# Second layer's convolution: offsets in two halves of the columns, the channel-major image in planes of contiguous tokens, the image scaled after its projection, expert masks made in pairs, base points moved

## The chip, the cores and the metric

One core of a Trainium2 chip runs the whole program. The metric is the device time of one execution in microseconds (us). The kernel before takes 274.34 us, the median of three runs (274.07 to 274.48). The engines are named as the profile names them: PE (TensorE, matmuls; PEld is its weight loads), DVE (VectorE), ACT (ScalarE), POOL (GpSimd), SP (SyncE, which here issues all DMAs).

## The reference, cut to what matters

A block of two layers works on x of 4 images, 16 x 16 tokens, 64 channels. Each layer is a deformable convolution and then a mixture of experts, each on a layer norm of its input and added to it. The change concerns the second layer's convolution and the steps on either side of it:

```
x = x + _L1_conv_ref(_ln_c(x), ...)          # _ln_c: (v - mean) / sqrt(var + 1e-6) over the channels
# inside _L1_conv_ref
x = conv_same(x, w_init, b_init)             # 1 x 1, 64 -> 64: "the image"
for g in range(4):                           # groups of 16 channels
    offsets = conv_same(xi, w_off[g], b_off[g])      # 3 x 3, 16 -> 18: nine points (x, y) for each token
    sampled = sample_with_offsets(xi, offsets, 3)    # bilinear, nine points for each token
    h = depthwise_same(sampled, w_dw[g], b_dw[g])
    outs.append(conv_same(h, w_pw[g], b_pw[g]))
```

Before it stands the first layer's mixture (eight experts, the two best weighted, gelu), after it the second's (the best expert alone, relu, with a capacity).

## The kernel before, in words

The 1024 tokens lie as 128 partitions x 8 columns (J = 8): a partition is half a row of an image, a column is one of the eight tokens of that half row. "Half" below means columns 0 to 3 or 4 to 7. Each engine runs its own hand-written list of instructions and meets the others at semaphores; nothing reorders a list. Where a helper records an operation, the profile gives the helper's line.

Around the change the order is this.

* First mixture. PE makes hidden rows (L840), broadcasts gate weights (L848), sums outputs (L862). ACT does the gelu (L645). DVE multiplies hidden rows by gates (L1425), sixteen times. Ahead of the sixteen, DVE adds the partition's position to the sampling base points (L1414, two instructions).
* Image. DVE adds the mixture's output to x in two halves (L1418), takes moments, POOL takes the power for the inverse deviation (L435), DVE normalises (L1128), PE transposes (L725), ACT copies. Then PE makes the image twice: channel-major in one matmul for each half (L910), copied by ACT and DVE into a padded picture (L251), and token-major (L754), copied by ACT in one piece (L660). SP stores it to a zeroed padded scratch in memory with four DMAs (L350) and reads back, with eight DMAs (L362), a window of five rows x twelve columns for each half row.
* Offsets. PE convolves the padded picture (L928: three taps for all tokens on 128 rows, three on 64 rows, in two blocks of 512 tokens). ACT adds the bias (L664), PE turns the result to tokens (L941).
* Weights. DVE adds base points, clips and subtracts (L1446 to L1451), ACT makes the linear tents (L669 to L676), DVE makes nine tables of weights, one for each of 3 x 3 neighbours (L282), each when its two factors are there. DVE then finishes a flag (L1145, L1146): if an offset is larger than one token, a general branch would run instead. It is not taken here.
* Sampling. Twelve items: four pairs of columns x three rows of sample points. For each item nine products of a slab and a table are summed. POOL makes six of the nine (L265, 72 in all), DVE three (L265, 36 in all). PE sums three of POOL's and one of DVE's in PSUM (L960), DVE adds the other five (L1555, L1559, L1564). POOL has eight slots for its products, and takes one again when PE or DVE has summed what lay there. PE then transposes the samples (L968) and applies the fused depthwise and pointwise weights (L978, L986).
* Second mixture. PE broadcasts one-hot masks (L1049), DVE masks the inputs (L1603), PE makes the hidden rows of the chosen expert (L1058), then outputs (L1098); DVE and POOL weigh and join them.

Some matmuls on zeros (L716, L708) compute nothing: `idle_columns` and `keep_clock` issue them so that PE is not idle. Thirty-two of them stand between L941 and the sampling.

Of the kernel before, what the change touches and what calls it, by code (L numbers as in the profile page):

```python
# [38 lines left out]
K = 9  # L39
# [31 lines left out]
def program(nc, a, out):  # L71
    ctx = ExitStack()
    with ctx:
# [13 lines left out]
        pad0, pad1 = scratch("pad0", R0), scratch("pad1", R1)  # L87
# [55 lines left out]
        w_i1 = sb("w_i1", P, 2, C)  # L143
# [99 lines left out]
        assert UE + G1 * UW <= BIG, UE + G1 * UW  # L243

        block = ctx.enter_context(nc.Block())

        def pad_image(copy, n):

            for hf in range(2):
                for b in range(B):  # L250
                    last = copy(V(cpad1, C * hf, b * NP0 + (W + 2) * (1 - hf) + 1 + HJ * n,  # L251
                                  [[1, C], [1, HJ], [W + 2, H], [HC, 2]]),
                                bank(4 + n, C * hf, C * hf + C, [P, HJ], [2, H], [1, 2], off=32 * b))
            return last
# [20 lines left out]
        def x_tents1(dx):  # L275

            return bank(4 + dx, 0, P, [1, J * GP1])

        def pair_weights(eng, d):

            dy, dx = divmod(d, 3)
            eng.tensor_tensor(bigv(AD + d * J * GP1, [1, J * GP1]), bigv(T1 + dy * J * GP1, [1, J * GP1]),  # L282
                              x_tents1(dx), ALU.mult).then_inc(sem("pairs"), 1)
# [22 lines left out]
        def _(sp):  # L306
# [14 lines left out]
            for pad, reach in ((pad0, R0), (pad1, R1)):  # L321
                n = B * (H + 2 * reach) * (W + 2 * reach) * C // P
                sp.dma_start(V2(pad, [[n, P], [1, n]]), zero[:, 0:n]).then_inc(sem("pad_zeroed"), 16)
# [8 lines left out]
            for i in range(2):  # L332
                load(w_i1[0:C + 1, i, :], "w_i1", "w_i1")
            load(w_of[:, 0, :], "w_of_a", "w_of")
            for hf in range(2):
                load(w_of[C * hf:C * hf + C, 1, :], "w_of_b", "w_of")
# [4 lines left out]
            load(b_tb[C:C + 1, :], "b_pw", "w_dp")  # L341

# [57 lines left out]
            sp.wait_ge(sem("img1"), 1)  # L400
            image_out(pad1, R1, "img1", "pad1_stored")
            slabs_in(pad1, R1, "pad1_stored", "slab1")
# [10 lines left out]
        def _(pool):  # L413
# [28 lines left out]
            for weights in (w_i1[:, :, :], cw_parts[:, :, :], oh_parts[:, :, :], b1_parts[:, :]):  # L442
                last = gp.memset(weights, 0.0)
# [29 lines left out]
            gp.memset(V(cpad1, 0, 0, [[1, P], [1, B * NP0]]), 0.0).then_inc(sem("cpad1_zero"), 1)  # L473
# [21 lines left out]
            pool.wait_ge(sem("w_of"), 64)  # L495
# [64 lines left out]
        def _(act):  # L560
            sc = nc.scalar

            def copy_T(k, halves=range(2)):

                for h in halves:
                    act.wait_ge(sem("xT_ps"), 2 * k + h - 1)
                    twice = {3: XT2, 5: XN2}
# [82 lines left out]
            for hf in range(2):  # L650
                act.wait_ge(sem("y0_ps"), hf + 1)
                sc.copy(bigv(Y0 + 512 * hf, [1, 512]), bank(4 + hf, 0, P, [1, 512])).then_inc(sem("yT0"), 1)
                if hf == 0:
                    copy_T(4, [0])

            act.wait_ge(sem("imgT_ps"), 1)
            pad_image(sc.copy, 0).then_inc(sem("cpad1"), 1)
            copy_T(4, [1])
            act.wait_ge(sem("img1_ps"), 2)
            sc.copy(V(img, 0, 0, [[1, P], [256, 2], [1, 256]]), bank(2, 0, P, [512, 2], [1, 256])).then_inc(sem("img1"), 1)  # L660
            act.wait_ge(sem("w_of"), 64)
            for n in range(2):
                act.wait_ge(sem("offT_ps"), n + 1)
                sc.activation(offT[:, 512 * n:512 * n + 512], bank(n, 0, 72, [1, 512]), ACT.Identity, bias=b_of[:, 0:1]  # L664
                              ).then_inc(sem("offT"), 1)

            NX = J * GP1
            act.wait_ge(sem("off1"), 1)
            sc.activation(x_tents1(2), u1[:, 0:NX], ACT.Relu).then_inc(sem("tent_x1"), 1)  # L669
            sc.activation(loc1[:, :], u1[:, :], ACT.Abs).then_inc(sem("abs1"), 1)  # L670
            act.wait_ge(sem("abs1"), 1)
            sc.activation(x_tents1(1), loc1[:, 0:NX], ACT.Relu, bias=1.0, scale=-1.0).then_inc(sem("tent_x1"), 1)
            sc.activation(x_tents1(0), u1[:, 0:NX], ACT.Relu, scale=-1.0).then_inc(sem("tent_x1"), 1)
            sc.activation(loc1[:, NX:2 * NX], loc1[:, NX:2 * NX], ACT.Relu, bias=1.0, scale=-1.0
                          ).then_inc(sem("tent_y1"), 1)
            sc.activation(ml[:, 0:NX], u1[:, NX:2 * NX], ACT.Relu, scale=-1.0).then_inc(sem("tent_y1"), 1)  # L676
# [10 lines left out]
            copy_raw_T(1)  # L687
            copy_T(5, [0])
# [3 lines left out]
            copy_T(5, [1])  # L692
# [8 lines left out]
        def _(pe):  # L701
# [17 lines left out]
            def transposes(k, src, ready, done_before, halves=range(2), m=C):  # L719

                pe.wait_ge(sem("ident"), 1)
                for h in halves:
# [4 lines left out]
                    if h == halves[0] and k in IDLE_BETWEEN:  # L727
                        idle_columns(*IDLE_BETWEEN[k])

            def gate_logits(src, ready, w, done_before):  # L730

                for h in range(2):
                    pe.wait_ge(sem(ready), h + 1)
# [1158 lines left out]
```

## Time and profile before

| | us |
|---|---|
| median of three runs | 274.34 |
| the profiled execution | 273.77 |
| its span, first to last instruction | 272.0 |
| PE busy | 230.9 (85%) |
| DVE busy | 191.2 (70%) |
| POOL busy | 136.6 (50%) |
| ACT busy | 60.2 (22%) |

The span leaves out 1.77 us of the profiled execution's time. The mean granted clock of TensorE is 0.986 of full speed. The shares of busy time are averages over stages that have different limits; the chain of work that ended last says, stage by stage, which engine the next step waited for.

### The profile page before, as it was taken

Reading aid. Unit: us, or ns where it says so; the run is one execution under the profiler, and the core shown is the slowest. Engines: PE = TensorE matmul, PEld = TensorE weight load, DVE = VectorE, ACT = ScalarE, POOL = GpSimd, SP = SyncE. Lnnn points to the kernel's source line nnn. Section 1 sums busy time; section 2 is a strip of 40 time slices with the busy share of each in tenths; the row PEclk is TensorE's granted clock in tenths of the full one; section 3 lists DMA queues with packets and bytes.
Section 4 is the critical chain, followed back from the end, with each engine's and each line's share of the span. In section 5 each row is a group of like instructions: output and inputs, shape, how many; then the busy total and the mean of one; then the engine's idle time right before and its main releaser. Section 6 shows DMA issues by size and latency. Waiting matters only on the chain.

```text
span 272.0 us, 3157 instructions
## 1 busy us (share of the span) xinstructions
PE 230.9 (85%) x1006; PEld 131.3 (48%) x1011; DVE 191.2 (70%) x480; ACT 60.2 (22%) x102; POOL 136.6 (50%) x195
## 2 busy tenths in 40 slices
PE   0999988987999979979798777789899988999980
PEld 0736467863345623224524233557577856434430
DVE  7797889997894886473506799898877138425486
ACT  1221953210001282614114000101001212311000
POOL 5400009885990619712600899999997002000760
PEclk9999999999999889999999999999999999999996
DMA  3526991000000000000059000000000000000000
GB/s 93 173 69 147 208 227 70 0 2 0 2 0 1 2 1 1 0 0 2 0 123 202 2 4 0 0 2 0 2 0 0 0 2 1 0 2 0 0 19 19
DMA packets 5760, 9.39 MB, mean 35 GB/s; under 512 B 2390, under 2 KB 2926, under 8 KB 5742
## 3 DMA queue, kind: packets, MB, share of 16 engines
q1 hardware_dynamic: 5742, 9.18, 14.5%
q8 instruction: 8, 0.13, 0.2%
q14 instruction: 10, 0.08, 0.1%
HBM read 7.48 MB, written 1.69 MB: 34 GB/s over the span
## 4 chain that ended last, share of the span: by engine, by line
PE 39%; DVE 30%; POOL 16%; issue 7%; ACT 6%; DMA 1%; DVEq 1%; ACTq 0%; POOLq 0%
POOL ring L265 13%; PE ps L1058 5%; PE ps L960 4%; PE ps L810 4%; DVE ps L1225 3%; PE ps L928 3%; PE ps L792 3%; PE ps L986 2%; DVE cm L1172 2%; DVE ring L289 2%; PE ps L725 2%; PE ps L862 2%; POOL big L554 2%; PE ps L840 2%; PE ps L978 1%
## 5 line engine op out<-in xcount | busy, mean ns | idle before, releaser
L265 POOL TENSOR_TENSOR ring<-big 128x384 f32<-128x384 f32 x72 | 57.7, 850 | 16.9 <-DMA big<-pad 16.5
L299 POOL TENSOR_TENSOR big<-big 128x512 f32<-128x512 f32 x30 | 31.9, 1092 | 34.7 <-DMA big<-pad 30.0
L960 PE MATMUL ps<-ring,ident 128*128 128x384 f32 x100 | 36.0, 499 | 8.4 <-POOL ring L265 5.6
L1555 DVE TENSOR_TENSOR ps<-ps,ring 128x384 f32<-128x384 f32 x46 | 25.8, 560 | 6.4 <-PE ps L960 5.1
L960 PEld LDWEIGHTS ps<-ring,ident 128*128 128x128 f32 x100 | 17.7, 190 | 23.1 <-DVE ring L265 5.0
L435 POOL TENSOR_TENSOR rstd<-veps,mhalf 128x4 f32<-128x4 f32 x8 | 8.2, 1027 | 38.9 <-DVE veps L1124 38.8
L792 PE MATMUL ps<-ring,ident 128*128 128x192 f32 x126 | 23.8, 337 | 3.8 <-DVE ring L289 3.6
L792 PEld LDWEIGHTS ps<-ring,ident 128*128 128x128 f32 x126 | 20.1, 190 | 7.6 <-DVE ring L289 7.6
L716 PE MATMUL ps<-zero 128*128 128x512 bf16 (+1 forms) x96 | 21.8, 372 | 0.3 <-issue 0.2
L554 POOL TENSOR_TENSOR big<-big 128x256 f32<-128x256 f32 (+1 forms) x12 | 7.6, 633 | 28.4 <-DVE big L1638 27.8
L265 DVE TENSOR_TENSOR ring<-big,ps 128x384 f32<-128x384 f32 x36 | 19.4, 545 | 0.1
L810 PE MATMUL ps<-ring,ident 128*128 128x512 f32 x30 | 14.8, 606 | 1.8 <-DVE ring L299 1.6
L289 DVE TENSOR_TENSOR ring<-big,ps 128x576 f32<-128x576 f32 x21 | 15.2, 745 | 1.2 <-ACT ps L610 1.1
L1058 PE MATMUL ps<-big,w 128*128 128x512 f32 x32 | 15.3, 612 | 0.0
L1225 DVE TENSOR_TENSOR ps<-ps,big 128x512 f32<-128x512 f32 x21 | 14.5, 692 | 1.0 <-POOL big L299 1.0
L682 ACT COPY big<-ps 128x512 f32<-128x512 f32 x8 | 4.6, 586 | 46.9 <-PE ps L968 46.9
L1425 DVE TENSOR_TENSOR big<-big,ps 128x512 f32<-128x512 f32 x16 | 10.2, 683 | 6.0 <-PE ps L848 2.4
L716 PEld LDWEIGHTS ps<-zero 128*128 128x128 bf16 x99 | 9.5, 99 | 9.6 <-issue 1.0
L1098 PE MATMUL ps<-w,big 128*128 128x512 f32 x32 | 13.9, 592 | 0.0
L725 PE MATMUL ps<-ident,xn 128*128 128x128 f32 (+1 forms) x32 | 5.9, 317 | 8.3 <-DVE xn L1128 8.2
L569 ACT COPY xT<-ps 64x512 f32<-64x512 f32 x6 | 3.4, 578 | 39.8 <-PE ps L725 39.8
L1603 DVE TENSOR_TENSOR big<-big,ps 128x512 f32<-128x512 f32 x8 | 5.5, 684 | 9.2 <-PE ps L1049 8.8
(282 smaller groups left out, 399.5 us busy)
## 6 DMA issues: line engine op xcount, KB each, us to landing
big<-pad SPq DMA_DIRECT2D x8, 392.0 KB, 9.7
big<-pad SPq DMA_DIRECT2D x8, 240.0 KB, 5.6
w<-in_w_dram SPq DMA_DIRECT2D x2, 512.0 KB
w<-in_w_dram SPq DMA_DIRECT2D x2, 256.0 KB
pad<-img SPq DMA_DIRECT2D x8, 64.0 KB, 2.1
pad<-zero SPq DMA_DIRECT2D x1, 484.0 KB, 3.8
pad<-zero SPq DMA_DIRECT2D x1, 400.0 KB, 4.3
x<-in_x_dram SPq DMA_DIRECT2D x1, 256.0 KB, 2.8
```

The lines of the kernel that those rows point to most:

```text
L265: return eng.tensor_tensor(V(ring, 0, slot * SP, [[1, P], [NJ * C, 3], [C1, NJ * G1], [1, C1]]), bigv((py + dy) * SLAB1 + (dx + j0) * C, [ ...
L289: eng.tensor_tensor(ring[:, slot:slot + J * GP0], bigv(TY + dy * J * GP0, [1, J * GP0]), x_tent, ALU.mult).then_inc(sem("a_dve"), 1)
L299: return eng.tensor_tensor(dst, bigv(wy * SLAB0 + wx * C, [C0, J * G0], [1, C0]), table, ALU.mult)
L554: step(gp.tensor_tensor(bigv(base, [1, half]), bigv(base, [1, half]), bigv(base + half, [1, half]), ALU.add))
L716: mm(bank(free_bank, 0, P, [1, width]), zeros[:, 0:P], zeros[:, 0:width], start=first, stop=first, skip_group_check=not first)
L792: return mm(bank(px + dx, 0, P, [1, 3 * J * G0], off=dy * J * G0), ident[:, :], ring[:, slot + 3 * px * J * G0:slot + 3 * (px + 1) * J * G ...
L810: mm(bank(7, 0, P, [1, 512]), ident[:, :], product, start=(n == 0), stop=(n == len(PE_SUMS) - 1)).then_inc(sem("acc0"), 1)
L960: mm(bank(1 + i % 2, 0, P, [1, SP]), ident[:, :], ring[:, slot * SP:slot * SP + SP], start=(n == 0), stop=(n == len(srcs) - 1)).then_inc(s ...
L1058: mm(bank(2 * hf + f, 0, P, [1, 512]), w_11[:, i, P * f:P * f + P], bigv(XM + 512 * u, [1, 512]), start=(i == 0), stop=False, skip_group_c ...
L1098: last = mm(bank(Y_BANKS[j % len(Y_BANKS)], 0, P, [1, E * C]), bigv(H1 + f * J * P + j * P, [1, P]), w_21[:, f, :], start=(f == 0), stop=( ...
L1225: v.tensor_tensor(dst, first, pool_slot(i, [1, 512]), ALU.add).then_inc(sem("v_sum"), 1)
L1555: v.tensor_tensor(acc, acc, ring[:, slot * SP:slot * SP + SP], ALU.add).then_inc(sem("s_add"), 1)
```

## The change

* **Image.** PE transposes x itself instead of its normalised form (`image_rows_T`), multiplies by `w_init` with its column means taken out (`image_rows`; the means are made once, beside those of the gates), and DVE scales the result by the inverse deviation and adds the bias on its way out of PSUM (`image_tokens`, four instructions for each half). The normalisation of x and ACT's copy L660 go. The image of half 0 is ready before that of half 1.
* **Channel-major image.** PE transposes the token-major image (`image_T`: for each column one transpose to partitions 0 to 63 and one matmul with the identity to partitions 64 to 127). ACT and DVE copy it into planes in which the 128 tokens of a column are contiguous (`upper_rows`, `lower_rows`, `middle_rows`); the copies carry the row shifts. POOL clears a second region for the middle rows.
* **Stores and windows.** SP stores each half of the image as it is ready (two DMAs each) and reads the windows as rows 0 to 2 (four DMAs) and rows 3 and 4 (four DMAs); POOL's first products wait only for the rows that they read.
* **Offsets in halves.** Six taps on 128 rows, each for columns 1 and 2 (`INNER`), 0 and 3 (`OUTER`), 4 to 7 (`SECOND`). The tokens of columns 0 to 3 are transposed while the taps of 4 to 7 run. DVE and ACT go through the whole chain of weights once for each half, with instructions of half the size; POOL's first six items wait only for half 0's tables.
* **Sampling.** For the first two items PE sums all six of POOL's products instead of three. The flag's transpose moves behind the first five sums. The 32 matmuls on zeros become four and ten.
* **Base points** move from ahead of the sixteen products into them (after the fourth and the sixth).
* **Expert masks** of the second mixture are issued two at a time, behind the hidden rows of the expert pair before.

The core of the diff:

```diff
@@ tensor: image and offsets
+                if k == HJ + 1:
+                    image_rows_T(0)
                 if k == HJ + 2:
-                    transposes(4, normalised, "xn", 2, [0])
+                    image_rows(0)
+                if k == HJ + 3:
+                    image_T(0, range(2))
-            image_by_channel(0)
             outputs_by_token(1)
-            keep_clock(4, 7)
-            transposes(4, normalised, "xn", 2, [1])
-            image_by_channel(1)
-            project(w_i1[0:C + 1, 0, :], 2, C, "img1_ps", 4)
+            image_T(0, range(2, HJ)).then_inc(sem("imgT_ps"), 1)
+            image_rows_T(1)
+            image_rows(1)
+            offset_taps(INNER, 0, 2)
+            image_T(1).then_inc(sem("imgT_ps"), 1)
+            offset_taps(INNER, 2, 6)
...
+            offset_taps(OUTER, 0, 6).then_inc(sem("offT_ps"), 1)
+            offset_taps(SECOND, 0, 2)
+            offsets_by_token(0)
+            offset_taps(SECOND, 2, 6).then_inc(sem("offT_ps"), 1)
+            idle_columns(4, 1)
+            offsets_by_token(1)
@@ tensor: sampling
+                    if i == 0 and n == S_POOL_PE(0) - 1:
+                        pe.wait_ge(sem("off_max"), 2)
+                        tr(bank(FLAG_BANK, 0, 1, [1, P]), flagf[:, 1:2], ident[:, :]).then_inc(sem("off_maxT"), 1)
+                        idle_columns(10, 6)
@@ tensor: second mixture
-                if u + 2 < E:
-                    expert_masks(u + 2)
                 chosen_hidden(u)
+                if u % 2 == 0 and u + 2 < E:
+                    expert_masks(u + 2)
+                    expert_masks(u + 3)
@@ scalar: biases of both halves, then the tents of both
             for n in range(2):
                 act.wait_ge(sem("offT_ps"), n + 1)
+                sc.activation(offT[:, 512 * n:512 * n + 512], bank(OFF_BANKS[n], 0, 72, [1, 512]), ACT.Identity,
+                              bias=b_of[:, 0:1]).then_inc(sem("offT"), 1)
+            for h in range(2):
+                act.wait_ge(sem("off1"), h + 1)
+                sc.activation(x_tents1(2, h), half1(u1, h), ACT.Relu).then_inc(sem("tent_x1"), 1)
...
@@ vector: weights of one half
+            for h in range(2):
+                both_val = half1(fx, h)
+                dve.wait_ge(sem("off1_ps"), h + 1)
+                step(v.tensor_tensor(V(loc1, 0, h * HJ * G1, cells), bank(2 + h, 0, P, [P, HJ], [G1, 2 * K], [1, G1]),
+                                     V(base1, 0, h * HJ * G1, cells), ALU.add))
+                v.tensor_scalar(val, loc, W - 1.0, None, ALU.is_lt).then_inc(sem("val1"), 1)
+                step(v.tensor_scalar(loc, loc, 0.0, W - 1.0, ALU.max, ALU.min))
+                v.tensor_tensor(off, loc, half1(base1, h, 0, 2 * K), ALU.subtract).then_inc(sem("off1"), 1)
...
@@ gpsimd
-            pool.wait_ge(sem("slab1"), 128)
+                    if i < 3:
+                        pool.wait_ge(sem("slab_top" if i % 3 + d // 3 < 3 else "slab_rest"), 16 * B)
                     if i == 0:
                         pool.wait_ge(sem("pairs"), PAIRS.index(d) + 1)
+                    if i == N_ITEMS // 2:
+                        pool.wait_ge(sem("pairs"), K + PAIRS.index(d) + 1)
@@ constants
-    return 3 if i < N_ITEMS - 2 else 4
+    return 6 if i < 2 else 3 if i < N_ITEMS - 2 else 4
```

## Rows read from the trace of the kernel before

**Rows 1.** Page, the chain that ended last: share of the span by line.

```profile
POOL ring L265 13%; PE ps L1058 5%; PE ps L960 4%; PE ps L810 4%; DVE ps L1225 3%; PE ps L928 3%; PE ps L792 3%; PE ps L986 2%; DVE cm L1172 2%; DVE ring L289 2%; PE ps L725 2%; PE ps L862 2%; POOL big L554 2%; PE ps L840 2%; PE ps L978 1%
```

**Rows 2.** The same chain in order of time: start us, us, what.

```profile
134.88 8.12 PE ps L928 x24
143.02 0.69 ACT fslab L664
143.76 1.12 PE ps L941 x8
...
155.76 0.40 DVE ps L272
...
161.17 34.34 POOL ring L265 x43
```

**Rows 3.** Timeline, POOL and SP: start us, us, engine line operation [idle before <-releaser].

```profile
134.98 2.47 SPq L350 DMA_DIRECT2D pad<-img  x4
138.93 5.07 SPq L362 DMA_DIRECT2D big<-pad  x8
...
150.94 9.02 POOL L265 TENSOR_TENSOR ring<-big 128x384 f32<-128x384 f32 x11 [16.54 <-DMA big<-pad]
160.25 48.81 POOL L265 TENSOR_TENSOR ring<-big 128x384 f32<-128x384 f32 x61 [0.28 <-DVE ps L1555]
```

**Rows 4.** Timeline, the chain of weights on DVE.

```profile
144.90 0.76 DVE L1446 TENSOR_TENSOR abx<-ps,base 128x576 f32<-128x576 f32 x1 [9.45 <-PE ps L941]
145.70 0.46 DVE L1449 TENSOR_SCALAR val<-abx 128x576 f32<-128x576 f32 x1
...
154.33 0.14 DVE L1146 TENSOR_SCALAR flagi<-flagf 1x1 int32<-1x1 f32 x1
```

**Rows 5.** Timeline in narrow windows, DVE instructions without and with POOL at work.

```profile
150.24 0.45 DVE L1468 TENSOR_TENSOR big<-abx,fx 128x288 f32<-128x288 f32 x1
151.83 1.07 DVE L1473 TENSOR_TENSOR big<-ml,fx 128x288 f32<-128x288 f32 x1
152.54 1.05 POOL L265 TENSOR_TENSOR ring<-big 128x384 f32<-128x384 f32 x1
101.51 1.12 DVE L1414 TENSOR_SCALAR base<-base,pf 128x288 f32<-128x288 f32 x1
```

**Rows 6.** Timeline, the start of the sixteen products of the first mixture.

```profile
101.25 1.22 POOL L489 MEMSET w_shift<- 128x1152 f32 x1 [5.74 <-DVE s_mask L1409]
...
101.95 1.48 PE L853 MATMUL ps<-cwT,b_parts 24*64 24x512 bf16 x6
...
104.00 0.10 PEld L848 LDWEIGHTS ps<-cwT,pick 128*128 128x128 bf16 x1 [0.50 <-DVE big L1425]
...
106.31 1.28 DVE L1425 TENSOR_TENSOR big<-big,ps 128x512 f32<-128x512 f32 x2 [1.13 <-PE ps L848]
```

**Rows 7.** Timeline, the image's stage.

```profile
121.38 1.27 DVE L1425 TENSOR_TENSOR big<-big,ps 128x512 f32<-128x512 f32 x2
...
124.69 1.00 PE L871 MATMUL ps<-both,big 128*128 128x64 f32 x8
...
132.37 1.90 PE L754 MATMUL ps<-w_i,xT 65*128 65x64 f32 x16
```

**Rows 8.** Timeline, DVE: the last sum of the third sampling item.

```profile
170.07 0.42 DVE L1559 TENSOR_TENSOR big<-ps,ring 128x256 f32<-128x256 f32 x1
```

**Rows 9.** Busy time by stretch: us, PE, PEld, DVE, ACT, POOL, PEclk, DMA share, GB/s.

```profile
94.00:96.00 2.00, 2.00 (x6) 0.97 (x8) 1.76 (x9) 0.26 (x1) 1.43 (x6) 0.50 0.00 0
```

**Rows 10.** Timeline, the masks and hidden rows of the second mixture.

```profile
229.95 0.69 DVE L1603 TENSOR_TENSOR big<-big,ps 128x512 f32<-128x512 f32 x1 [0.39 <-PE ps L1044]
...
231.81 0.37 PE L1049 MATMUL ps<-cwT,pick_half 8*128 8x512 bf16 x1 [1.19 <-ACT cwT L690]
232.12 1.98 PE L1058 MATMUL ps<-big,w 128*128 128x512 f32 x4
...
250.19 13.90 PE L1098 MATMUL ps<-w,big 128*128 128x512 f32 x32
```

More of the change, by code:

```diff
@@ L243, in program, with lower_rows, upper_rows, middle_rows @@
         assert UE + G1 * UW <= BIG, UE + G1 * UW
+        MIDDLE = ST
         block = ctx.enter_context(nc.Block())
[L247 to L254, printed above, removed]
+        def lower_rows(copy, n):
+            copy(V(cm, 0, (1 + HJ * n) * P + 2, [[1, C], [P, HJ], [32, B], [1, 30]]),
+                 bank(4 + n, 0, C, [P, HJ], [32, B], [1, 30]))
+            side, src = ((J + 1) * P + 2, 1) if n == 0 else (3, (HJ - 1) * P)
+            return copy(V(cm, 0, side, [[1, C], [32, B], [2, 15]]),
+                        bank(4 + n, 0, C, [32, B], [2, 15], off=src))
+        def upper_rows(copy, n):
+            copy(V(cm, C, (1 + HJ * n) * P, [[1, C], [P, HJ], [32, B], [1, 30]]),
+                 bank(4 + n, C, P, [P, HJ], [32, B], [1, 30], off=2))
+            side, src = ((J + 1) * P, 3) if n == 0 else (1, (HJ - 1) * P + 2)
+            return copy(V(cm, C, side, [[1, C], [32, B], [2, 15]]),
+                        bank(4 + n, C, P, [32, B], [2, 15], off=src))
+        def middle_rows(copy, n):
+            copy(bigv(MIDDLE + (1 + HJ * n) * P, [1, HJ * P], p=C), bank(4 + n, 0, C, [1, HJ * P]))
+            side, src = ((J + 1) * P, 1) if n == 0 else (1, (HJ - 1) * P)
+            return copy(bigv(MIDDLE + side, [2, P // 2], p=C), bank(4 + n, 0, C, [2, P // 2], off=src))
         def sample_product(eng, i, d, slot):
@@ L653, in _ @@
                 if hf == 0:
[L654 to L661, printed above, removed]
+                    copy_image_T(0)
+                else:
+                    act.wait_ge(sem("cpad1_zero"), 1)
+                    act.wait_ge(sem("imgT_ps"), 1)
+                    upper_rows(sc.copy, 0).then_inc(sem("outer"), 1)
@@ L662, in _ @@
+            copy_image_T(1)
+            act.wait_ge(sem("imgT_ps"), 2)
+            upper_rows(sc.copy, 1).then_inc(sem("outer"), 1)
+            act.wait_ge(sem("w_of"), 48)
             for n in range(2):
                 act.wait_ge(sem("offT_ps"), n + 1)
[L664 to L675, printed above, removed]
@@ L726, in transposes, with gate_logits @@
                     last.then_inc(sem("xT_ps"), 1)
[L727 to L730 removed]
+            def gate_logits(src, w, done_before):
                 for h in range(2):
[L733 removed]
+                    pe.wait_ge(sem("x_sum"), 2 * done_before + h + 1)
                     for j in range(HJ * h, HJ * h + HJ):
@@ L1478, in _ @@
+            flag_finish(1, FLAG_BANK, 1.0, ALU.is_gt)
             flag = dve.value_load(flagi[0:1, 1:2], min_val=0, max_val=1)
-            dve.wait_ge(sem("pairs"), len(PAIRS))
+            dve.wait_ge(sem("pairs"), 2 * len(PAIRS))
+            for _, _, arrived in SLAB_PARTS:
+                dve.wait_ge(sem(arrived), 16 * B)
             with dve.If(flag > 0):
@@ L1726 @@
 DVE_TENTS = 2
-T_PLACE = {(5, 1): 3}
-IDLE_BETWEEN = {}
+T_PLACE = {(4, 1): 3}
+TENT_BANKS = ((4, 5, 6), (3, 0, 7))
+FLAG_BANK = 4
+TILE = J + 2
+OFF_BANKS = (6, 0)
+INNER, OUTER, SECOND = (1, 1, 2, 1), (0, 3, 2, 2), (HJ, 1, HJ, 2)
+SLAB_PARTS = ((0, 3, "slab_top"), (3, 2, "slab_rest"))
 HIDDEN_AT = {1: (4,), 2: (5, 6), 3: (7,)}
```

264 lines of the change are left out of this document (154 added, 110 removed).

## The prediction

> **What bounds the kernel now.** I read the page's chain first: no line has more than 13% of the span, and the one that has it is POOL's sampling product, L265 [rows 1]. So the second step is the chain in order of time around the sampling [rows 2]: the offset taps on PE (134.88 to 143.00), ACT's bias, the turn to tokens, DVE's weights, DVE's first sampling instruction at 155.76, some DVE sums, and from 161.17 POOL for 34 us. The third is POOL's own timeline [rows 3]: it waits 16.54 us for the windows, makes eleven products from 150.94, is held 0.28 us by a DVE sum, and runs the other 61 without a gap, one every 48.81 / 61 = 0.80 us. So POOL sets the length of the sampling and two things set its start: the windows' arrival, and how soon DVE and PE free its eight slots. The product that starts at 160.25 waited for DVE, though POOL had begun 4.8 us ahead of it. **DVE's start, not POOL's, is what has to move.** The last view is DVE and POOL side by side [rows 5]; it decides the sum.
>
> Times below are on the clock of the trace of before; the shift of the first part is taken off at the end.
>
> **Base points.** L1414 leaves the place ahead of the sixteen products. PE then no longer waits at 104.00 for DVE, but goes on at the end of L853, 103.43 [rows 6]: about 0.55 us for all that follows. Moved behind the fourth and the sixth product, they lie in DVE's waits for PE, 1.13 us at the first such place [rows 6]; without that cover they cost what L1414 does, up to 1.12 each [rows 5]. POOL's second clearing is about as long as L489, 1.22 us, and lies ahead of a wait of 5.74 us [rows 6]. The mean of `w_init` adds one small instruction each to PE and DVE ahead of L725: nothing to 0.2 us, taken as nothing.
>
> **Image and taps.** DVE loses four normalising instructions, so the sixteenth product ends at about 121.75 instead of 122.65 [rows 7]; PE fills that time with `image_rows(0)`, half of L754's 1.90, and `outputs_by_token(1)` stays where L871 is, 124.69 to 125.69 [rows 7]. From there, one thing waiting for the next (short steps, estimated by size from L664, L941, L1446 and L754 [rows 2, 4, 7]): DVE's sum 0.45, four transposes 0.45 behind the rest of `image_T(0)`, ACT's copy 0.6 behind `upper_rows` (to 127.8), `image_rows(1)` 1.0, four scalings behind DVE's plane copies 0.95 (to 129.75), twelve short passes of `image_T(1)` 1.35: 131.1. Then PE alone. L928's 24 passes took 8.12 us with twelve of them two at a time, so one pass of 512 columns is 8.12 / 18 = 0.45 [rows 2], of 256 columns 0.225. Rest of `INNER` 1.8, biases 0.6, `OUTER` 2.7 (136.2), two of `SECOND` 1.8, four turns 0.55 (half of L941), the rest 3.6: 142.1. Half 0's offsets leave PE 6.8 us earlier than all did, half 1's 0.9 earlier. But in ACT's list half 1's bias (0.69, L664 [rows 2]) stands ahead of half 0's tents, so half 0's first tent comes at 142.9 + 0.3 and its first table at about 143.5. The windows: the second half's image is in SBUF at 129.75, its stores take some 3.6 us from there as L350's do to L362's first issue (134.98 is when they began, 138.93 when the loads did [rows 3]), the eight loads take 12.0 us from first issue to POOL's start [rows 3], and rows 0 to 2 are three fifths of them: about 133.4 + 7.2 = 140.6, rows 3 and 4 at 145.4, ahead of product 6. So **POOL starts at 143.6 instead of 150.94**.
>
> **DVE's weights in halves.** Half the columns is not half the time: 576 columns take 0.76, 288 take 0.45 [rows 4, 5], so 144 take about 0.3. Were DVE alone, half 0 would end at 147.3 and half 1 at 153.3, and the sampling would start 1.3 + 0.4 us later (L1146 to L272, with the flag's reduction [rows 2, 4]): 155.0. But POOL is now at work beside it. L1473, two inputs in SBUF, took 1.07 where its twin L1468 took 0.45: it stood until POOL's second product was over, and POOL's third, queued at 152.54, took 1.05 instead of 0.80 because it stood in turn [rows 5]. The second L1414, a scalar instruction from SBUF, took 1.12 beside L489, which ended at 102.47 [rows 5, 6]. In the chain of half 1, five instructions in a row are of these kinds (two scalar, subtraction, product of validities, first y tent), then two y tents, as are two in half 0. After each of them POOL's queued product goes first, so the next one waits a product less the time it was late: I take 0.3 and 4 x 0.8 for the five, 0.35 on average for each of the other four: 4.9 us. Bounds: nothing (no instruction here is shown in a row of such) and 9 x 0.85 = 7.7. I take 4.9, near L1473's 0.62 each. The nine tables (L282) take one factor from PSUM and are not counted. So DVE's first sampling instruction comes at 155.0 + 4.9 = **159.9, taken as 159.5** for pauses of POOL, against 155.76.
>
> The Trainium skill, "SBUF — State Buffer", section "Who interferes with whom", says that a VectorE instruction with two SBUF inputs, or in a mode that uses both ports, and a GpSimd instruction shut each other out for their whole length, the one that issues first going first. By that rule, which speaks against starting POOL amid DVE's weights, each of the nine can wait up to a whole product; the trace agrees at the one place that shows it, L1473's 1.07 against 0.45.
>
> **Sampling.** DVE needed 170.07 - 155.76 = 14.3 us from its first instruction to the end of item three [rows 2, 8]. PE now takes six of its sums (two items x three), at a pitch of half a product and sum, 0.47: 2.8 less; PE adds seven instead of four per item, on which DVE waits 0.2: 11.7. The slot of POOL's product 25 comes free 0.7 later, at 159.5 + 12.4 = 171.9. Before, that product started at 160.25 + 14 x 0.80 = 171.45. POOL's 7.3 us of earlier start are spent: after fourteen products it has no slot until PE has DVE's first product. With the 0.55 from the base points: 171.35, **0.1 earlier than before**. From there on both are paced by POOL.
>
> **Masks in pairs.** The first hidden rows waited for masks that wait for ACT (231.81) and began at 232.12, though their input was there at 230.64 [rows 10]. Now they begin at 230.7: 1.4 less. Two masks in a row save 0.1 each time, the hidden rows behind them take as long; the transposes move behind both masks, 0.3 more. L1098 starts at 248.85 instead of 250.19: **1.35 us**, all on the path, since DVE is ready earlier by as much.
>
> **Sum.** 0.1 + 1.35 = 1.45 us. The profiled execution would take 273.77 - 1.45 = 272.3 (span 270.55); it lies 0.57 below the median of the runs, so the forecast is 274.34 - 1.45 = 272.9 us, with 271.5 to 274.2 for its own small terms.
>
> **Rivals.**
> * *DVE and POOL hardly hold each other.* For: POOL's products beside PSUM-reading DVE instructions keep their pace [rows 3]; against: L1473. DVE starts at 155.0; product 25 is then set by POOL's own start, its two stops for slots (2.7 us) and its pace, some 4.5 us earlier than forecast: 268.4.
> * *TensorE's clock falls in the image's stage*, whose filler is gone and whose passes are short. In the trace the clock stood at 0.50, the lower level of 1.2 GHz, in 94 to 96 [rows 9], behind short transposes and the eight-column matmuls of the gates. Some 3.4 us at that level cost 1.7 of PE's chain, which moves DVE's start by as much: 274.6.
> * *Each of the nine waits a whole product*, 7.7 instead of 4.9 us: DVE starts at 162.3, and 272.9 + 2.8 = 275.7, slower. It turns at 6.35 us in all, 0.7 for each; L1473's 0.62 stands just below. That the change doesn't do what it says belongs here: POOL begins early and ends no earlier.
>
> **How the numbers follow.** Forecast 0.50, first rival 0.20, second 0.16, third 0.14. The time is the forecast's. Range 268.4 to 275.7: it takes in the first rival's end and the third's, and leaves out clocks and waits together, and gains beyond. A measurement of this kernel tells about 0.2% (0.55 us) from no change. Faster: four fifths of the forecast's cases and the first rival, 0.60; within: 0.18, from the forecast's upper edge and half of the second; slower: 0.22.
>
> **What would show it.** Right: POOL's first product near 143, DVE's first sampling instruction after 158, DVE instructions with two SBUF inputs in half 1 at 0.9 to 1.1 us instead of 0.3 to 0.45, POOL idle before its fifteenth and sixteenth products, its last product ending within 1 us of 209.1, L1098 starting 1.3 us closer to it. Wrong: half 1's instructions at their lone durations, a clock below 1.00 in 124 to 135, or windows later than the first table.

## The result

| | before | after |
|---|---|---|
| median of the runs, us | 274.34 | 276.17 |
| ratio to before, 95% interval | 1 | 1.0077 [1.0045, 1.0108] |
| span of the profiled execution, us | 272.0 | 275.1 |
| TensorE's mean granted clock in it | 0.986 | 0.969 |

The forecast was 272.9 us, with 268.4 to 275.7 as its range and 0.60 on "faster". By this measurement the change is 0.8% slower, clear of no change, and the time lies outside the range; a second measurement, further down, gives 0.3%. A few executions of the kernels measured here are slower throughout; the ratios leave them out, the medians do not.

The first view after is the chain in order of time around the sampling, as in [rows 2]: start us, us, what.

```profile
158.75 0.40 DVE ps L288
159.17 0.56 DVE ring L281
159.78 8.54 PE ps L1034 x16
```

The stretch from 159.78 is new. In [rows 2] the chain went from DVE's first sampling instruction (155.76) over DVE's own sums to POOL; now it stands for 8.54 us in eight sums on PE (each sum is two records). POOL's timeline says the same from the other side, to be laid beside [rows 3]:

```profile
144.90 12.03 POOL L281 TENSOR_TENSOR ring<-big 128x384 f32<-128x384 f32 x14 [10.21 <-DVE big L302]
162.85 0.84 POOL L281 TENSOR_TENSOR ring<-big 128x384 f32<-128x384 f32 x1 [5.92 <-PE ps L1034]
165.61 4.93 POOL L281 TENSOR_TENSOR ring<-big 128x384 f32<-128x384 f32 x6 [1.92 <-PE ps L1034]
171.06 1.63 POOL L281 TENSOR_TENSOR ring<-big 128x384 f32<-128x384 f32 x2 [0.51 <-PE ps L1034]
174.58 39.25 POOL L281 TENSOR_TENSOR ring<-big 128x384 f32<-128x384 f32 x49 [1.89 <-DVE ps L1657]
```

POOL begins at 144.90 instead of 150.94, six microseconds earlier, and then gives 5.92 + 1.92 + 0.51 + 1.89 = 10.24 us back at four stops. Its last product ends at 213.83; before, at 160.25 + 48.81 = 209.06. DVE's row for the first sum of item one (168.34; items are numbered from zero) names who holds it. The timeline of DVE also shows its first instruction on half 0's offsets (140.03) and the last large sum of item two (175.53):

```profile
140.03 0.46 DVE L1548 TENSOR_TENSOR abx<-ps,base 128x288 f32<-128x288 f32 x1 [3.88 <-PE ps L964]
...
158.75 0.39 DVE L288 COPY ps<-big 128x216 f32<-128x216 f32 x1 [1.39 <-issue]
161.46 0.57 DVE L1657 TENSOR_TENSOR ps<-ps,ring 128x384 f32<-128x384 f32 x1 [0.81 <-PE ps L1034]
168.34 0.57 DVE L1657 TENSOR_TENSOR ps<-ps,ring 128x384 f32<-128x384 f32 x1 [4.22 <-PE ps L1034]
171.66 0.57 DVE L1657 TENSOR_TENSOR ps<-ps,ring 128x384 f32<-128x384 f32 x1 [0.66 <-PE ps L1034]
175.53 0.42 DVE L1661 TENSOR_TENSOR big<-ps,ring 128x256 f32<-128x256 f32 x1
```

DVE waits 0.81 + 4.22 + 0.66 = 5.69 us for PE in three items. One reason is in the stretches, columns as in [rows 9], and in PE's own row behind them:

```profile
156.00:158.00 2.00, 0.06 (x1) 0.00 (x0) 1.30 (x6) 0.00 (x0) 0.93 (x2) 1.00 0.00 0
158.00:160.00 2.00, 0.22 (x1) 0.22 (x2) 1.21 (x3) 0.00 (x0) 0.00 (x0) 0.76 0.01 4
160.00:162.00 2.00, 2.00 (x4) 0.95 (x4) 1.19 (x4) 0.00 (x0) 0.00 (x0) 0.50 0.00 0
159.78 9.17 PE L1034 MATMUL ps<-ring,ident 128*128 128x384 f32 x18 [3.72 <-DVE ring L281]
```

PE stood idle from 156.06, the end of its fillers, to 159.78; inside that gap the granted clock fell to 0.50, and the sums that everybody waits for ran at the lower level of 1.2 GHz, one every 1.07 us (8.54 / 8).

The end of the kernel went the other way: POOL's last product to L1177, which is L1098 of [rows 10].

```profile
253.30 13.90 PE L1177 MATMUL ps<-w,big 128*128 128x512 f32 x32
```

That is 253.30 - 213.83 = 39.47 us, against 250.19 - 209.06 = 41.13.

So the span's 3.1 us split into three stretches. To L921, the first turn of outputs into tokens (L871 before): 116.31 against 116.48, -0.17. From there to POOL's last product: 97.52 against 92.58, +4.94. From there to the end: 275.1 - 213.83 = 61.27 against 62.94, -1.67.

### The profile page after: what moved, and what is told of

Same layout as the page of the kernel before. It is cut to its first block, busy times and chain, and to the rows that moved or that the text cites. A ratio compares the mean times of both kernels' runs of the same rounds, so it can differ in the third digit from the quotient of the medians.

```text
span 275.1 us, 3237 instructions
## 1 busy us (share of the span) xinstructions
PE 236.9 (86%) x1031; PEld 135.4 (49%) x1031; DVE 194.2 (71%) x492; ACT 59.6 (22%) x103; POOL 138.3 (50%) x196
## 4 chain that ended last, share of the span: by engine, by line
PE 48%; DVE 25%; POOL 11%; ACT 7%; issue 7%; DMA 1%; DVEq 1%; ACTq 0%; POOLq 0%
POOL ring L281 9%; PE ps L1034 7%; PE ps L1136 5%; PE ps L954 4%; PE ps L858 4%; PE ps L890 3%; DVE ps L1304 3%; PE ps L840 3%; PE ps L912 2%; PE ps L1064 2%; DVE cm L1251 2%; DVE ring L309 2%; PE ps L775 2%; POOL big L598 2%; PE ps L766 2%
## 5 line engine op out<-in xcount | busy, mean ns | idle before, releaser
L281 POOL TENSOR_TENSOR ring<-big 128x384 f32<-128x384 f32 x72 | 58.5, 852 | 20.6 <-DVE big L302 10.2
L1034 PE MATMUL ps<-ring,ident 128*128 128x384 f32 x112 | 43.1, 529 | 8.4 <-DVE ring L281 5.1
L1034 PEld LDWEIGHTS ps<-ring,ident 128*128 128x128 f32 x112 | 21.1, 202 | 26.2 <-DVE ring L281 8.5
L1657 DVE TENSOR_TENSOR ps<-ps,ring 128x384 f32<-128x384 f32 x40 | 22.5, 562 | 10.9 <-PE ps L1034 9.6
L840 PEld LDWEIGHTS ps<-ring,ident 128*128 128x128 f32 x126 | 20.1, 190 | 7.2 <-DVE ring L309 7.2
L766 PE MATMUL ps<-zero 128*128 128x512 bf16 (+1 forms) x81 | 18.6, 370 | 0.0
L1524 DVE TENSOR_TENSOR big<-big,ps 128x512 f32<-128x512 f32 x16 | 10.2, 684 | 5.4 <-PE ps L898 4.0
L1177 PE MATMUL ps<-w,big 128*128 128x512 f32 x32 | 13.9, 592 | 0.0
L890 PE MATMUL ps<-big,w 64*128 64x512 f32 x32 | 10.8, 780 | 1.6 <-ACT big L694 1.0
L766 PEld LDWEIGHTS ps<-zero 128*128 128x128 bf16 x81 | 7.8, 98 | 8.2 <-issue 1.7
L319 DVE TENSOR_TENSOR ring<-big,ps 128x512 f32<-128x512 f32 x15 | 10.2, 678 | 2.0 <-ACT big L683 2.0
L694 ACT ACTIVATE big<-ps,b 128x512 f32<-128x512 f32 x16 | 9.9, 688 | 5.3 <-PE ps L890 5.3
```

The lines of the kernel that those rows point to most:

```text
L281: return eng.tensor_tensor(V(ring, 0, slot * SP, [[1, P], [NJ * C, 3], [C1, NJ * G1], [1, C1]]), bigv((py + dy) * SLAB1 + (dx + j0) * C, [ ...
L319: return eng.tensor_tensor(dst, bigv(wy * SLAB0 + wx * C, [C0, J * G0], [1, C0]), table, ALU.mult)
L766: mm(bank(free_bank, 0, P, [1, width]), zeros[:, 0:P], zeros[:, 0:width], start=first, stop=first, skip_group_check=not first)
L840: return mm(bank(px + dx, 0, P, [1, 3 * J * G0], off=dy * J * G0), ident[:, :], ring[:, slot + 3 * px * J * G0:slot + 3 * (px + 1) * J * G ...
L890: mm(bank(2 * (k % 2) + n, 0, F0, [1, 512]), w_10[C * n:C * n + C, F0 * i:F0 * i + F0], V(big, C * n, XT2 + 512 * hf, [[1, C], [1, 512]]), ...
L1034: mm(bank(1 + i % 2, 0, P, [1, SP]), ident[:, :], ring[:, slot * SP:slot * SP + SP], start=(n == 0), stop=(n == len(srcs) - 1)).then_inc(s ...
```

## The experiments

Two theories and two rivals stood. Theory one: the lowered clock in 158 to 165. Theory two: TensorE's seven sums one behind the other, at any clock. The rivals: DVE's late start beside POOL; and the six sums moved to PE as such. Code lines in the text are those of the kernel after; in the rows of an edited kernel the same lines can have numbers a few higher or lower. Executions of one kernel also differ ahead of the sampling (the same code reaches L921 between 114.68 and 117.16, with the clock lowered for some of 92 to 104 or not), so kernels are compared below by a distance within one profile: from DVE's first instruction on half 0's offsets (L1548) to the end of POOL's last product. For the kernel after it is 213.83 - 140.03 = 73.80.

**More fillers.**

```diff
-                        idle_columns(10, 6)
+                        idle_columns(22, 6)
```

> The kernel after with 22 instead of 10 matmuls on zeros behind the turn of the flag (153.74 to 156.06 after; 12 more at 0.23 us end at 158.9, ahead of the 159.78 at which TensorE has its next work). Theory (the clock, lowered in 158.5 to 165, doubles TensorE's fifteen sums of the first items): granted clock 1.00 in 157 to 170, eight sums from 159.8 in about 4.5 us instead of 8.54, POOL's last product ends near 210 instead of 213.8, median near 272.3. Rival 1 (VectorE's late start beside POOL is the cause): the clock is 1.00 but the time stays within 1 us of 276.2. Rival 2 (seven sums an item are too many for TensorE at any clock): 275 or more, VectorE's first sum of item one still after 167.

Measured: ratio 1.0009 [0.9968, 1.0050], 276.15 us beside 275.31 of the kernel before on that chip. Rows of the timelines of POOL and DVE, and one stretch:

```profile
162.20 0.84 POOL L281 TENSOR_TENSOR ring<-big 128x384 f32<-128x384 f32 x1 [4.55 <-PE ps L1034]
164.22 4.83 POOL L281 TENSOR_TENSOR ring<-big 128x384 f32<-128x384 f32 x6 [1.18 <-PE ps L1034]
172.93 39.28 POOL L281 TENSOR_TENSOR ring<-big 128x384 f32<-128x384 f32 x49 [1.89 <-DVE ps L1657]
166.69 0.57 DVE L1657 TENSOR_TENSOR ps<-ps,ring 128x384 f32<-128x384 f32 x1 [2.60 <-PE ps L1034]
173.88 0.42 DVE L1661 TENSOR_TENSOR big<-ps,ring 128x256 f32<-128x256 f32 x1
160.00:162.00 2.00, 1.51 (x4) 0.68 (x4) 1.93 (x5) 0.00 (x0) 0.00 (x0) 1.00 0.02 4
```

The clock stays at 1.00, the distance is 212.21 - 140.73 = 71.48, 2.3 us less. By time the gain is less clear: the ratio is 1.0009 here, against 1.0077 and, in the second measurement, 1.0031 of the kernel after, and the intervals overlap. Either way the change comes level with the kernel before and no further: DVE still waits 2.60 us for PE's seven sums at item one. The lowered clock is about half of the miss between the profiles (4.55 us, worked out below), and the first theory expected all of it.

**Three sums instead of six.**

```diff
-    return 6 if i < 2 else 3 if i < N_ITEMS - 2 else 4
+    return 3 if i < N_ITEMS - 2 else 4
```

> The kernel after with three instead of six of POOL's products left to TensorE in items zero and one (the six sums go back to VectorE); the turn of the flag and its ten fillers then stand behind TensorE's third sum. Theory (clock): TensorE has even less to do, the clock falls still, but TensorE has four sums an item to do at it, some 4.2 us, beside VectorE's 4.7: 274.5 to 276, POOL's product of the twenty-fourth place at 173 to 174. Rival 2 (the six sums on TensorE are the loss by themselves): the sampling goes as before the change, 272.5 to 273.5. Rival 1 (VectorE's start): 276 or more, since VectorE starts at the same 158.75 and has six sums more.

Measured: ratio 1.0047 [1.0007, 1.0088], 276.04 us. POOL:

```profile
144.94 9.50 POOL L281 TENSOR_TENSOR ring<-big 128x384 f32<-128x384 f32 x11 [10.21 <-DVE big L302]
162.66 48.81 POOL L281 TENSOR_TENSOR ring<-big 128x384 f32<-128x384 f32 x61 [8.22 <-DVE ps L1657]
```

Distance 211.47 - 140.06 = 71.41: as with six sums at the full clock. The clock fell here too, earlier (0.50 in 153 to 158), where PE had only fillers to run. One long stop for DVE took the place of four short ones. So at the full clock the six sums gain nothing in the order that the change gives them, and lose nothing either; the rival that they are the loss by themselves falls.

**POOL begins only when all tables are made.**

```diff
                     if i == 0:
-                        pool.wait_ge(sem("pairs"), PAIRS.index(d) + 1)
+                        pool.wait_ge(sem("pairs"), 2 * K)
```

with the turn of the flag moved ahead of the sums, between 22 and 9 fillers.

> The kernel after with POOL's first product waiting until all eighteen tables are made, and 22 + 9 fillers around the turn of the flag, which goes ahead of the sums: nothing runs on POOL beside VectorE's weights. Theory of the hold: half 1's instructions with two inputs in SBUF or with a scalar take 0.3 to 0.45 instead of 0.87 to 0.98, VectorE's first sampling instruction at 155.0 instead of 158.75. POOL then starts near 153.6 and paces all from there: its product of the twenty-fourth place at about 172.5 (174.58 after), last product at 211.7, median about 274. Were there no hold, VectorE would start at 158.75 as after, and the time would be over 277.

Measured: ratio 0.9970 [0.9940, 1.0000], 273.70 us. Two instructions of DVE in the kernel after, then the same two and DVE's and POOL's start in this run:

```profile
149.24 0.94 DVE L1552 TENSOR_SCALAR abx<-abx 128x288 f32<-128x288 f32 x1
150.21 0.98 DVE L1553 TENSOR_TENSOR aby<-abx,base 128x288 f32<-128x288 f32 x1
...
148.38 0.30 DVE L1552 TENSOR_SCALAR abx<-abx 128x288 f32<-128x288 f32 x1
148.72 0.46 DVE L1553 TENSOR_TENSOR aby<-abx,base 128x288 f32<-128x288 f32 x1
154.84 0.39 DVE L288 COPY ps<-big 128x216 f32<-128x216 f32 x1 [1.39 <-issue]
153.27 57.44 POOL L281 TENSOR_TENSOR ring<-big 128x384 f32<-128x384 f32 x72 [18.57 <-DVE big L302]
```

With POOL silent, L1552, L1553 and L1555 took 0.30, 0.46 and 0.30 instead of 0.94, 0.98 and 0.94, and DVE began its sampling at 154.84 instead of 158.75, with the same first instruction (140.04 and 140.03): **the hold costs DVE 3.91 us**. Eight instructions are longer beside POOL, one of half 0 and seven of half 1, by 0.13 to 0.67 us each, 3.89 in all. POOL started 8.4 us later than after and made its 72 products without a stop. The distance is 210.71 - 140.04 = 70.67, 0.8 below that of the run with more fillers (the clock was at 1.00 in both). So in this order of PE's sums an early start that is spent on waiting for slots, and holds DVE meanwhile, is worth nothing.

**The fillers of the kernel before cut to the numbers of after**, 4 + 10 for 26 + 6.

> The kernel before with its 26 + 6 fillers between the offsets' turn and the sampling cut to 4 + 10, the numbers of the kernel after. Theory (clock): the granted clock falls to 0.50 somewhere in 150 to 162, TensorE's sums of item zero and one take 1.0 instead of 0.55 us, and the time is 0.7 to 2.5 us over the kernel before, 275 to 276.8. Rivals 1 and 2: no fall and no change, within 0.4 us of 274.3.

Measured: ratio 0.9995 [0.9960, 1.0030], 274.40 us. A stretch and POOL's row (line of the kernel before):

```profile
150.00:153.00 3.00, 1.83 (x5) 0.70 (x6) 2.97 (x8) 0.63 (x2) 1.20 (x2) 0.50 0.14 26
161.11 48.81 POOL L265 TENSOR_TENSOR ring<-big 128x384 f32<-128x384 f32 x61 [0.28 <-DVE ps L1555]
```

The clock fell as expected and cost nothing, which was not expected: POOL's stop is 0.28 as in [rows 3]. The fall came earlier than in the kernel after, and the kernel before has nothing on PE that others wait for in that stretch (by 156 to 158 the clock was at 1.00 again). This run alone does not show what a fall under PE's sums costs in the kernel before; the run with the masks in pairs, below, does.

**TensorE's order.** Item zero's six POOL products, the flag (which stands behind six sums in the kernel after too, not behind five), item one's six, then DVE's products of both, instead of DVE's product of item one in second place among its seven (the tables of slots and counts follow):

```diff
+    if i == 0:
+        return [s for s in both if s[2] == "pool"] + [s for s in both if s[2] == "dve"]
```

> The kernel after with TensorE's order changed for the first two items: the six products of POOL for item zero, the flag, the six of item one, and only then VectorE's products of items zero and one. In the kernel after TensorE cannot sum item one's POOL products until VectorE's product of item zero and then of item one are there, and VectorE's first sum of item one waits for all seven. Theory (TensorE's seven sums one behind the other are the loss, whatever the clock): VectorE waits under 0.7 us for TensorE at item one, POOL stops at most 1.5 us in all between its fourteenth and its twenty-fourth product, the twenty-fourth starts near 168 instead of 174.6, last product ends near 207.5, median 269 to 271.5. Rival (the lowered clock is the loss, the order is not): the time stays over 274.

Measured: ratio 0.9915 [0.9879, 0.9951], 272.99 us. POOL, and DVE's last large sum of item two:

```profile
145.03 16.81 POOL L281 TENSOR_TENSOR ring<-big 128x384 f32<-128x384 f32 x20 [10.21 <-DVE big L302]
163.58 0.84 POOL L281 TENSOR_TENSOR ring<-big 128x384 f32<-128x384 f32 x1 [1.74 <-PE ps L1033]
166.14 1.63 POOL L281 TENSOR_TENSOR ring<-big 128x384 f32<-128x384 f32 x2 [1.72 <-PE ps L1033]
169.66 39.25 POOL L281 TENSOR_TENSOR ring<-big 128x384 f32<-128x384 f32 x49 [1.89 <-DVE ps L1656]
170.62 0.42 DVE L1660 TENSOR_TENSOR big<-ps,ring 128x256 f32<-128x256 f32 x1
```

Twenty products without a stop instead of fourteen; DVE no longer waits for PE at item one. The distance is 208.91 - 140.16 = 68.75, 5.0 us less than after. The clock was at 1.00 here with the ten fillers of the kernel after, and PE went on with item one's sums at 156 without a gap; so 2.3 of the 5.0 are the clock's and 2.7 are the order's. The 2.3 is that of the run with more fillers, so the split is a difference of single profiles; two profiles of the kernel after differ by 0.2 in the distance. The three stops that remain, 5.35 us in all, wait for sums of item two.

**Positions in PSUM.** Half 1's positions, cut positions and product of validities are kept in PSUM, with the product taken from the positions:

```diff
-                step(v.tensor_scalar(loc, loc, 0.0, W - 1.0, ALU.max, ALU.min))
-                v.tensor_tensor(off, loc, half1(base1, h, 0, 2 * K), ALU.subtract).then_inc(sem("off1"), 1)
+                step(v.tensor_scalar(cut, loc, 0.0, W - 1.0, ALU.max, ALU.min))
+                v.tensor_tensor(off, cut, half1(base1, h, 0, 2 * K), ALU.subtract).then_inc(sem("off1"), 1)
```

> The kernel after with half 1's positions, cut positions and product of validities in PSUM, so that no instruction of half 1's weights between the offsets and the tables reads two inputs from SBUF or is a scalar instruction from SBUF; all the rest, POOL's early start too, as after. Theory of the hold: these instructions take 0.3 to 0.5 us instead of 0.87 to 0.98 beside POOL, VectorE's first sampling instruction comes at 155.3 to 156 instead of 158.75, and the time falls by as much, to about 273. Were the lengths those of crowding by POOL in general, they would stay at 0.9 and the time at 276.

Measured: ratio 0.9965 [0.9926, 1.0004], 273.81 us. DVE and POOL:

```profile
148.61 0.46 DVE L1557 TENSOR_SCALAR ps<-ps 128x288 f32<-128x288 f32 x1
149.10 0.46 DVE L1558 TENSOR_TENSOR aby<-ps,base 128x288 f32<-128x288 f32 x1
155.20 0.39 DVE L288 COPY ps<-big 128x216 f32<-128x216 f32 x1 [1.39 <-issue]
144.31 11.42 POOL L281 TENSOR_TENSOR ring<-big 128x384 f32<-128x384 f32 x14 [10.20 <-DVE big L302]
```

POOL works beside these instructions as in the kernel after, and they take 0.30 to 0.46; POOL's fourteen products take 11.42 instead of 12.03. So POOL's work alone does not lengthen DVE's; it depends on what DVE reads. DVE starts 155.20 - 139.43 = 15.77 after its first instruction instead of 18.72, 2.95 of the 3.91 us. Of the rest, 0.67 is half 0's one instruction, which was not edited and still takes 0.97 instead of 0.30; two scalar instructions that now read PSUM take 0.46 where they took 0.30 from SBUF with POOL silent. POOL's last product ends at 207.91, so the distance is 207.91 - 139.43 = 68.48; the clock was at 1.00 in this profile as well, so some 3.0 of the 5.3 us are the hold's. The Trainium skill, "SBUF — State Buffer", section "Who interferes with whom", says that a VectorE instruction with at most one SBUF input and outside the two-port modes doesn't contend with GpSimd; these rows agree.

**Both edits together.**

> The two edits of the runs on TensorE's order and on the positions in PSUM together. If each is a cause of its own: VectorE's first sampling instruction at 155.3 to 156, POOL's 72 products without a stop of more than 0.5 us from 144.9, at 0.80 to 0.84 each, last product near 204 to 206, median 265 to 269. If one of them only hides the other: no more than 0.5 us below the better of the two.

Measured: ratio 0.9810 [0.9751, 0.9868], 270.98 us. POOL, and one stretch ahead of the sampling:

```profile
104.00:144.00 40.00, 38.01 (x173) 17.12 (x173) 19.57 (x58) 9.77 (x18) 17.50 (x27) 0.96 0.23 52
147.09 17.13 POOL L281 TENSOR_TENSOR ring<-big 128x384 f32<-128x384 f32 x21 [11.54 <-DVE big L302]
165.94 1.64 POOL L281 TENSOR_TENSOR ring<-big 128x384 f32<-128x384 f32 x2 [1.72 <-PE ps L1033]
169.47 39.24 POOL L281 TENSOR_TENSOR ring<-big 128x384 f32<-128x384 f32 x49 [1.89 <-DVE ps L1665]
```

Distance 208.71 - 142.21 = 66.50: 2.25 and 1.98 below the two edits alone, so each is a cause of its own. The expected 265 to 269 was missed: the two stops at item two (3.61 us) stayed. In this profile the clock also stood at 0.50 for some 3.4 us of 130 to 134, in the image's stage (0.63 in 130 to 132, 0.51 in 132 to 134), and L921 to DVE's first instruction took 142.21 - 117.16 = 25.05 us instead of 140.03 - 116.31 = 23.72. The two of the six executions with the highest mean clock, 0.994, took 268.63 and 269.15.

**The kernel before with only the masks in pairs.**

> The kernel before with only the masks in pairs. By the forecast's own step: 1.35 us less, the first hidden rows start 1.3 us earlier behind POOL's last product, about 273.0 beside 274.3. Rival (the hidden rows wait for the transposes that now stand behind two masks): within 0.4 us of the kernel before.

Measured: ratio 0.9938 [0.9908, 0.9969], 273.34 us. A stretch, POOL and PE (lines of that kernel, where L1099 is L1098 of before):

```profile
160.00:162.00 2.00, 2.00 (x4) 1.18 (x4) 2.00 (x6) 0.00 (x0) 1.66 (x3) 0.50 0.00 0
161.51 48.81 POOL L265 TENSOR_TENSOR ring<-big 128x384 f32<-128x384 f32 x61 [0.34 <-DVE ps L1556]
249.80 13.90 PE L1099 MATMUL ps<-w,big 128*128 128x512 f32 x32
```

249.80 - 210.32 = 39.48 against 41.13: 1.65 us, and the time falls by 0.6%: this part of the change is a gain by itself. The stretch shows something else: here the clock was at 0.50 under PE's sums of the first items, as in the kernel after, and POOL's stop is 0.34 us instead of 0.28. In the kernel before DVE and POOL hardly wait for these sums (DVE 0.30 us at 163.32 instead of 0.21); a lowered clock has its price where PE is on the path.

**The kernel after once more, unchanged.**

> The kernel after, unchanged, a second time, for its profile: in its first profile the granted clock was 0.50 around 158 to 165, and a kernel of the same fillers (TensorE's order changed) kept 1.00 there. If the lowered clock belongs to the change, it is there again, POOL's stop ahead of its fifteenth product is 5.9 us and VectorE waits 4.2 us for TensorE at item one. If it comes and goes, a profile without it shows the stop near 4.5 us and the wait near 2.6, as with 22 fillers, the end 2.3 us earlier; the remaining loss against the kernel before is then the order of TensorE's sums alone. Time 275.5 to 277.5.

Measured: ratio 1.0031 [0.9999, 1.0063], 276.43 us. The first measurement gave 1.0077 [1.0045, 1.0108]. The change is no gain by either; by this one its loss is just not clear of no change. Rows of POOL and DVE, and one stretch:

```profile
161.24 0.84 POOL L281 TENSOR_TENSOR ring<-big 128x384 f32<-128x384 f32 x1 [5.92 <-PE ps L1034]
172.70 39.29 POOL L281 TENSOR_TENSOR ring<-big 128x384 f32<-128x384 f32 x49 [1.89 <-DVE ps L1657]
166.46 0.57 DVE L1657 TENSOR_TENSOR ps<-ps,ring 128x384 f32<-128x384 f32 x1 [3.96 <-PE ps L1034]
158.00:160.00 2.00, 1.84 (x3) 1.17 (x4) 1.19 (x4) 0.00 (x0) 0.00 (x0) 0.50 0.00 0
```

The clock fell at the same place, in the same gap of 3.72 us on PE, though it stayed at 1.00 in 92 to 104 this time (L921 at 114.68). The distance is 211.99 - 138.41 = 73.58, 0.22 below the first profile's. In both profiles of the change the fall is there.

**Item two as well**, on top of both edits: its six POOL products to PE, into a bank of their own, so that no earlier item has to be finished (three of them ahead of DVE's product of item one; the tables for that order are not shown).

```diff
-    return 6 if i < 2 else 3 if i < N_ITEMS - 2 else 4
+    return 6 if i < 3 else 3 if i < N_ITEMS - 2 else 4
```

> The run of both edits (TensorE's order, positions in PSUM), and the same for item two: all six of its POOL products are summed by TensorE, into a bank of their own, so that they wait for no item before. In the run of both POOL still stood 1.72 us for TensorE's sum of item two and 1.89 us for VectorE's (3.6 us in all), though TensorE and VectorE had time. If POOL alone is then the bound: its 72 products without a stop of more than 0.5 us, 58 to 59 us from first start to last end, and 3 us less than the run of both, median 267 to 269. If VectorE is the bound behind it (its sums of items three to eleven at 4.7 us each): POOL's stops only move to later items, and the gain is under 1 us.

Measured: ratio 0.9717 [0.9679, 0.9755], **267.87 us** beside 275.33 of the kernel before on that chip.

```profile
145.88 23.52 POOL L281 TENSOR_TENSOR ring<-big 128x384 f32<-128x384 f32 x29 [11.50 <-DVE big L302]
170.86 34.46 POOL L281 TENSOR_TENSOR ring<-big 128x384 f32<-128x384 f32 x43 [1.47 <-DVE ps L1665]
```

One stop is left; the 72 products take 59.44 us, and the distance is 205.32 - 141.00 = 64.32, 9.5 us less than after. The stop of 1.47 us was to be under 0.5: DVE's sums of item three are what POOL meets next.

## Why the prediction was wrong

**The step that failed** is in the part on the sampling: "PE adds seven instead of four per item, on which DVE waits 0.2: 11.7." The forecast counted from DVE's first sampling instruction to the start of the last large sum of the third item (170.07 is that row's start), and so does this comparison: 175.53 - 158.75 = 16.78 us after, 173.88 - 159.46 = 14.42 with the clock held up by more fillers, and 170.62 - 158.88 = 11.74 with TensorE's order changed (158.75, 159.46 and 158.88 are DVE's first sampling instructions). Of the 5.08 us by which the term is too small, 2.36 are the clock, 2.68 the order, and 0.04 remain. The pitch of DVE's products and sums was right, the wait was not: after, DVE's sum waits for *all seven* of an item, DVE's own product stands second among PE's seven and is made only behind DVE's first sum of the item ahead, and PE's other five sums of item one stand behind that product, so DVE waits for them in a row, 2.60 us even at the full clock. POOL's twelfth product, the last of item one, had been ready since about 155.2 (144.90 + 12 x 0.86); only PE's order kept them from being summed. The clock's share has a second source: the change takes 18 of 32 fillers away just ahead of these sums, and that edit had no price in the working.

The other steps, in the order of the prediction:

* **What bounds the kernel** held: DVE's start had to move, and POOL's early start alone did nothing (the run without the hold starts POOL 8.4 us later and is faster).
* **Base points**: -0.55 forecast, -0.17 at L921. PE's wait for DVE is gone, but in the first profile after the clock stood at 0.50 in 96 to 100 (0.85 before), so PE came late to the gates by itself. In the two profiles at 1.00 throughout 92 to 104, the second one of the kernel after and that of the positions in PSUM, L921 comes at 114.68 and 115.72. What the edit is worth by itself is not shown. The second L1496 took 2.18 us beside POOL, more than the 1.12 forecast at most and over its cover of 1.13, and yet L912 at 104.16 to L921 is 12.15 us, as from L862 at 104.33 to L871 before: hidden.
* **Image and taps**: 1.5 us short, counted from L921 (before: from L871, 116.48). Four columns of `image_T(1)` take 2.35 us (0.59 for each), not 1.35, and the taps ended 143.4 - 116.3 = 27.1 us behind it instead of 142.1 - 116.5 = 25.6. POOL began 28.6 us behind it in both profiles of the kernel after; 143.6 - 116.48 = 27.1 was forecast. Windows were no wait, DVE's first table was. (From the first store to the first load the rows of before give 138.93 - 134.98 = 3.95 us, not 3.6; this decided nothing.)
* **DVE's weights in halves**: right, in part by luck. With POOL silent DVE's first sampling instruction was forecast 155.0 - 116.48 = 38.5 us behind L921, and came 154.84 - 116.31 = 38.5 behind it, though the taps and so the first table were 1.5 late: the chain from there on was forecast as much too long. The hold was 4.5 in the forecast (4.9 in its working) and 3.91 measured, over eight instructions instead of nine; none waited a whole product longer. In all, 158.95 was forecast and 158.75 measured.
* **Masks**: 1.35 forecast, 1.65 to 1.67 measured.
* **First rival** (hardly any hold, 0.20): falls, three instructions at 0.94 to 0.98 say so. **Third rival** (each of nine waits a whole product, 7.7): falls, 3.91. Its time, 275.7, lies nearest to the measured 276.17, but by chance: the loss lies behind DVE's start, not ahead of it. What it says beside that, that POOL begins early and ends no earlier, came true.
* **Second rival** (the clock falls, 0.16): the mechanism came, in the kernel after in another place. It was looked for in the image's stage, where the clock stayed at 1.00 in 104 to 144 in both its profiles, and it fell between the offsets and the sampling. In the profiles of two edited kernels with the same image stage it fell there too (both edits together, and item two as well: 0.96 in 104 to 144, some 3.4 us at 0.50), and L921 to DVE's first instruction took 25.05 and 25.01 us instead of 23.72, 1.3 us more; the rival had 1.7.

Summed up, the profiled executions miss the forecast by 3.1 + 1.45 = 4.55 us: 4.49 between L921 and POOL's last product (4.94 instead of 0.55 - 0.1 = 0.45), 0.38 ahead of it, -0.32 behind it. Between the medians it is 3.3 (276.17 against 272.9), since the profiled execution of after lies 0.69 above its median and that of before 0.57 below.

## What to carry to other kernels

When sums move from a busy engine to an idle one, ask not only how many it can do but in which order its queue holds them: work that is ready is of no use behind an operand that is made late (2.7 us here). Filler that is taken out has to be priced wherever its engine is on the path next, since a fall of the clock under the same sums cost 2.3 us here and under 0.1 at POOL's stop in the kernel before. And an early start of the engine that paces a stage counts only as far as its buffers are emptied: extend the emptying (order, bank, one more item) together with the start.

## What the runs showed of the hardware that was not expected

* The price of the hold, and what it hangs on. The forecast had whole products for a chain of such instructions, 0.8 us each; eight scalar and two-input instructions that read SBUF took 0.43 to 0.98 beside POOL instead of 0.30 to 0.46 without it. With one operand in PSUM those of half 1 took 0.30 to 0.46 while POOL's products went on at 0.82 each. L1561, a reduction of one SBUF operand, took 0.74 beside POOL and 0.75 alone.
* What decides whether the clock falls stays open. It fell in both profiles of the kernel after behind a gap of 3.72 us on PE, and not in the run with positions in PSUM behind a gap of 2.90; but in the kernel before with the masks in pairs it stood at 0.50 in 160 to 162 behind a gap of only 2.24, where the kernel before, with a gap of 2.23 at the same place, kept 1.00. In the image's stage of the two profiles named above it fell behind short passes, with no gap on PE longer than 0.86 us, where the kernel after, with the same instructions, kept 1.00. No run here tells these apart.
